# Both parts of the divided values made directly behind the division, in the narrow causal attention layers of a macaron block

## What is computed

```python
def _L0_ffn_ref(x, ln_w, ff_ln_w, wq, wk, wv, wo, wg, w1, w3, w2):
    ...
    q = (h @ wq).reshape(B, S, NHEADS, HEAD_DIM)      # 32 heads of 64
    k = (h @ wk).reshape(B, S, KVHEADS, HEAD_DIM)     # 8 of 64
    v = (h @ wv).reshape(B, S, KVHEADS, HEAD_DIM)
    q, k = _rope(q, k)
    ...
    scores = jnp.where(causal[None, None], scores, jnp.float32(-1e+30))
    attn = jax.nn.softmax(scores, -1)
    o = jnp.einsum('bhqk,bhkd->bqhd', attn, v).reshape(B, S, NHEADS * HEAD_DIM)
    x = x + o @ wo
    ...
```

## Time and profile before

| | us |
|---|---|
| median of three runs | 4106.93 |
| lowest, highest | 4098.98, 4127.73 |
| the profiled execution | 4071.79 |
| its span, first to last instruction | 4070.0 |
| busy: TensorE, VectorE, ScalarE, GpSimd | 3419.7, 2315.2, 1920.3, 1151.3 |
| mean granted TensorE clock | 0.906 of full |

### The profile page before, as it was taken

How to read it: one execution, slowest core, us unless ns; L and a number is a source line. 1 busy time by engine, 2 the same in 40 slices (tenths; PEclk the granted TensorE clock), 3 DMA queues, 4 the chain that set the end, 5 groups by cost and what they waited for, 6 DMA issues and landing times. The chain is left out here.

```text
span 4070.0 us, 63736 instructions
## 1 busy us (share of the span) xinstructions
PE 3419.7 (84%) x21128; PEld 2262.4 (56%) x21130; DVE 2315.2 (57%) x7805; ACT 1920.3 (47%) x5261; POOL 1151.3 (28%) x1088
## 2 busy tenths in 40 slices
PE   6898889888698698988788898888779766999976
PEld 4566666665354333333556666665445445788864
DVE  5555555555343577774555555556434367777765
ACT  4565656645222056666456665655422113555541
POOL 3222322243344200011222222234345442222213
PEclk9899999988799688989899999999889877999996
DMA  2022233011654422120102332311275610000010
GB/s 70 24 68 94 97 125 114 26 56 59 191 90 83 110 52 52 25 43 13 29 23 66 125 114 84 109 32 59 79 182 90 131 38 1 14 14 4 1 31 21
DMA packets 226444, 268.79 MB, mean 66 GB/s; under 512 B 25478, under 2 KB 196424, under 8 KB 225352
## 3 DMA queue, kind: packets, MB, share of 16 engines
q1 hardware_dynamic: 195176, 224.58, 18.1%
q0 software_dynamic: 30944, 40.14, 5.8%
HBM read 129.59 MB, written 134.25 MB: 65 GB/s over the span
## 5 line engine op out<-in xcount | busy, mean ns | idle before, releaser
L1786 ACT ACTIVATE p_prob<-bank,p_small 128x256 f32<-128x256 f32 (+3 forms) x1280 | 646.7, 521 | 151.3 <-DVE p_small L1961 144.2
L1961 DVE CUSTOM_DVE_ANT_0 bank<-bank,p_mask 128x256 f32<-128x256 f32 (+3 forms) x1280 | 581.5, 487 | 240.1 <-PE bank L1525 237.5
L1791 ACT ACTIVATE p_prT<-bank 128x512 f32<-128x512 f32 x752 | 420.4, 602 | 349.9 <-PE bank L1534 349.9
L1525 PE MATMUL bank<-p_k,p_q 64*128 64x256 f32 (+3 forms) x3840 | 537.1, 354 | 10.3 <-ACT p_prob L1786 9.2
L1534 PE MATMUL bank<-g_ident,p_prob 128*128 128x128 f32 x3008 | 431.6, 288 | 68.8 <-DVE p_q L1946 20.7
L2330 POOL TENSOR_TENSOR p_oT_lo<-p_oT,p_oT_hi 128x512 fp32r<-128x512 f32 x128 | 162.3, 1268 | 1068.3 <-ACT p_oT_hi L1799 1057.9
L1534 PEld LDWEIGHTS bank<-g_ident,p_prob 128*128 128x128 f32 x3008 | 339.8, 145 | 152.9 <-DVE p_q L1946 52.7
L1543 PE MATMUL bank<-p_prT,p_v 128*64 128x512 f32 (+1 forms) x1504 | 418.7, 601 | 0.3 <-ACT p_prT L1791 0.3
L1525 PEld LDWEIGHTS bank<-p_k,p_q 64*128 64x128 f32 (+1 forms) x3840 | 346.9, 194 | 113.4 <-issue 70.9
L2319 POOL TENSOR_TENSOR p_tm<-p_rope_a,p_rope_b 128x512 f32<-128x512 f32 x192 | 246.8, 1286 | 517.1 <-DVE p_rope_b L1941 491.6
L2020 DVE TENSOR_REDUCE p_nmax<-bank 128x1 f32<-128x512 f32 x512 | 324.9, 683 | 101.4 <-PE bank L1588 95.7
(11 more groups left out here) (296 smaller groups left out, 6626.8 us busy)
## 6 DMA issues: line engine op xcount, KB each, us to landing
sorted<-p_blank SPq DMA_DIRECT2D x32, 2304.0 KB, 13.1
p_oT<-inverse_saved SPq DMA_DIRECT2D x256, 128.0 KB, 2.9
p_w<-in_L_ffn_w SPq DMA_DIRECT2D x96, 256.0 KB, 4.3
p_h_in<-sorted SPq DMA_DIRECT2D x158, 144.0 KB, 2.7
p_k_st<-k_saved SPq DMA_DIRECT2D x16, 288.0 KB
p_q_st<-q_saved SPq DMA_DIRECT2D x16, 288.0 KB
g_stage<-in_L_ffn_wq SPq DMA_DIRECT2D x8, 512.0 KB, 4.6
g_stage<-in_L_ffn_wo SPq DMA_DIRECT2D x16, 256.0 KB, 6.2
```

Source lines behind the costliest of these rows:

```text
L1525: ins = pe.matmul(h.use.ap[:, 0:n], q[rows, at, :], k[rows, kp, o.g, keys], start=i == 0, stop=i == 2)
L1786: act.activation(s.prob.ap[:, 0:s.o.w], s.use.ap[:, 0:s.o.w], ACT.Exp, bias=sm[:, 0, j:j + 1], scale=-1.0, accum_out=sm[:, 1, j:j + 1]).th ...
L1791: act.activation(s.prT.ap, s.use.ap, ACT.Copy).then_inc(s.use.free[0].sem)
L1961: dve.tensor_tensor_reduce(x, x, A.mask[:, A.mask.shape[1] - o.w:], -1.0, FAR, ALU.add, ALU.min, o.sm.ap[:, 0, h.j:h.j + 1]).then_inc(made)
```

## The change

The step "parts" moves from behind the turns of the first two key tiles to directly behind "divide". The two calls of beside(), the projection of the row tile before (not in the same iteration: `settled` is None there), the scores of heads 2 and 3 and the turns stood between them.

```diff
@@ -626,7 +626,9 @@
                     beside()
                 exponentials()
                 if weighed:
-                    (low_parts if wide else divide)(weighed)
+                    if not wide:
+                        divide(weighed)
+                    low_parts(weighed)
                 if wide:
                     scores(cur, 1)
                 else:
@@ -641,8 +643,6 @@
                     scores(cur, 2, 3)
                 for kt in range(0, min(2, nturn)):
                     turn(prev, kt)
-                if weighed and not wide:
-                    low_parts(weighed)
                 exponentials()
                 if wide:
                     scores(cur, 2)
```

## The result

| | before | after |
|---|---|---|
| Time, us | 4105.7 (4099.0 to 4127.7, 4 runs) | 3994.1 (3989.9 to 4005.8, 4 runs) |
| The profiled execution, us (span) | 4071.8 (4070.0) | 3989.9 (3988.1) |
| Time on a second chip, us | 4061.0 (4053.5 to 4073.2, 9 runs) | 3959.6 (3954.7 to 3970.0, 5 runs) |
| The profiled execution there, us (span) | none taken | 3956.7 (3954.9) |

The change makes the kernel faster: ratio 0.972 (0.968 to 0.977), 112 us, and 0.9755 (0.973 to 0.978) on the second chip, 101 us. Forecast were 78 us and 4029 us in a range of 4000 to 4080: the direction was right, the gain was over two fifths larger, and 3994 lies 6 us under the range.

The account below looks back on a forecast made before the run. TensorE's order was taken to set the pace, its idle stretches being winnable: 117.7 us of waits less 9.4, 5.4, 4, 4.3, 4.2 and 17 gave 73, plus 4 for the clock 77, scaled to 78: 4029 us, range 4000 to 4080.

Parts of the forecast that it names:

- What TensorE waits for: Before the output projection, TensorE waits for the low part, late because ScalarE makes the high part late: 117.7 us, 94 times.
- Position 0's next wait: At the division called position 0, the projection still waits for its bank: 0.8 of 1.28 us won, 4.3 us off the sum.
- The loss at position 2: In 24 units of the first three column blocks, the held q copy delays TensorE's last turn 0.71 us: 17 us lost.
- Rival 3: ScalarE, held by 78 late divisions, becomes what TensorE waits for: at 60% passed on, 28 us slower, 4135 us; chance 0.06.
- The term of the clock: Five low-clock stretches (0.50) follow ordinary position 3 waits, each costing up to 1.7 us: 4 us taken, bound 8.5.
- What a wait is worth: TensorE's waits before the projection were counted at their waiting time, 117.7 us before deductions, with no term for the first matmul.
- The fourth block: At position 2 in the fourth column block, the router's scaling on VectorE holds TensorE anyway: 0 us taken.
- Position 1: The projection's wait of 0.74 us goes, but the q copy limits the win to 0.6 us a unit.
- The idle time itself: TensorE's waits at the projection, 117.7 us, less what stays and the position 2 loss: 73 us won.
- Scaling the sum: The 77 us gain on the profiled run was scaled to the runs' median, 0.86% higher: 78 us.
- The prediction's own sign of being wrong: A narrow causal layer that isn't 35 to 40 us shorter would show the prediction wrong.
- Rival 2: Position 2 costs nothing and all low-clock stretches behind position 3 go: 99 us won, 4007 us; chance 0.13.

Follow-up runs that it names:

- the pair without the stretches: First profile of the kernel before against the changed kernel's on chip B, neither with VectorE or ScalarE standing idle in the fourth blocks; spans differ by 115.1 us.
- the kernel with the copies first: Changed kernel with the parts at position 2 behind the q and k copies, ahead of the scores: 3979.2 us on chip A, 3949.8 us on chip B.
- the pair with the stretches: Also "the pair on A": second profile of the kernel before, on chip A, against the profile after, both with fourth-block idle stretches; 109.1 us less in the narrow layers.

## Why the prediction was right in kind and too small

Right, by its own steps:

- *What TensorE waits for.* The low part was late because ScalarE made the high part behind other copies. With the high part in its new place 84 of 94 waits go, and moving ScalarE's part alone gives the whole gain (3989.9 us).
- *Position 0's next wait.* 0.56 us for the bank of the last rotation; 0.5 was in the sum.
- *The loss at position 2.* The q copy starts 0.69 us later (0.71 reckoned) and the k low part 0.68, so the chain runs as told; but TensorE's wait for it grows by 0.45 us in this unit, to 0.93 and not to 1.2. That ScalarE takes its instructions strictly in order (the Trainium skill, TensorE: Matmul & The Clock Gate, Architectural detail) agrees with this row; it is a cost only where somebody is waiting for what is held.
- *Rival 3*, which needs the holding behind late divisions to reach TensorE: a kernel that holds 0.6 us longer everywhere pays 13 to 22 us.

Wrong, and by how much, in the pair without the stretches (104.7 us measured in the narrow layers, 77 reckoned):

- **The term of the clock**, 4 us with a bound of 8.5. It is the step that failed most. It measured about 20 us in both pairs. The prediction counted five spells behind ordinary position 3 waits; these are the ones in the first three column blocks behind a wait of 1.5 us. The trace of the kernel before has nine behind position 3 waits of 1.5 us or more, and the changed kernel has none, on either chip. So all of them went, and other short ones with them: of spells of 3.4 and 6.8 us there were 23 and are 11, of the longer ones 9 and 10 (on A 25 and 17, 8 and 8). At position 3 alone the time at 0.50 fell by 31 of the 44 us, and TensorE's busy time there by 15. A kernel's time at 0.50 is no measure of its time by itself: the kernel with the copies first has 10 us more of it than the changed one on B, and the same busy time.
- **What a wait is worth**, taken as its idle time alone. The first matmul behind a wait adds 0.26 us more than without one. That term was put at nothing, and it gave about 17 us at the projection and 12 net.
- **The fourth block.** The two fourth blocks together won 31 us. Their idle time fell by 18.4, which is what the sum's waits in them make with the last unit's taken off (14 to 19), and their busy time by 12.4. Position 2 there was taken as 0, because the router's scaling holds TensorE, and won 6.7. A part of that is seen: before the change GpSimd's subtraction ran there at the same time as an instruction of the router on VectorE (L2146), which then took 1.13 us instead of 0.19 and ended with it, and the k low part and TensorE's router step (L1694) stood behind:

```profile
806.09 1.26 POOL L2330 TENSOR_TENSOR p_oT_lo<-p_oT,p_oT_hi 128x512 fp32r<-128x512 f32 x1 [7.88 <-ACT p_oT_hi L1799]
806.27 1.13 DVE L2146 TENSOR_TENSOR p_n_tiles<-p_n_tiles 128x32 f32<-128x32 f32 x1
...
808.09 0.17 PE L1694 MATMUL bank<-p_n_tiles,g_earlier 128*128 128x16 bf16 x1 [3.33 <-DVE p_k L1951]
```

This happens three times in the first profile of the kernel before and one to six times in every kernel whose parts at position 2 stay late in the fourth block, and never in the seven profiles of kernels whose parts there come earlier. TensorE's wait at L1694 for the k low part falls from 14.6 to 10.9 us (on A 18.2 to 10.9, and 14.8 with position 2 alone late).
- **Position 1**, 0.6 us a unit: the q low part moved by 0.90, since the q copy, too, stands behind the projection. In the first three blocks 0.79 us a unit were won, 0.48 of it idle time and 0.31 the projection's first matmul.
- **Position 2 in the first three blocks**: 17 reckoned, 13.5 measured here, 7 in the pair with the stretches.

The idle time itself came out as summed (72.3 against 73), which is partly luck: position 3 gave 35 us of it (39 reckoned) and position 1 15 (20), and position 2 lost 8 and not 17. In the pair on A it fell by 86. In the runs the prediction was for, the gain is 112 us. Scaling the sum by 4106.9/4071.8 was no help: the 35 us between profile and median were not a longer version of the same work but stretches in two blocks that the profile did not have.

The prediction's own sign of being wrong, a narrow layer that isn't 35 to 40 us shorter, came true: from the first to the last division the layers are 55.7 and 49.0 us shorter. The range failed by 6 us. Rival 2 (position 2 free, all low clock gone, 99 us) named the right direction and the right term, but its bound for the clock, 8.5 us, capped it, and position 2 was not free. With a bound from all of the 205 us at 0.50 the range would have begun below 3990.

What stays open: where the stretches of the fourth blocks come from; the rest of what position 2 wins there; and why the waits that went took just these spells at the low clock with them. No run holds the waits and the clock apart.

## What to carry to other kernels

When a change takes short waits out of TensorE's queue at regular places, reckon three things: the idle time; what the first matmul behind each wait adds (here 0.26 us); and the granted clock over the whole stretch, with all the time at the low level as the bound and not a count of a few spells. A wait moved onto an in-order engine costs what its readers lose and not what it holds, so look for the reader first. And when a profile's own time lies outside the range of the timed runs, find out what it lacks before scaling by the median.

## What the runs showed of the hardware

Two chips ran the same kernel 0.9% apart (4099 and 4061 us; two sets on the one, one on the other), at much the same granted clock (about 0.91 over the span on both). The difference lies in the fourth column block of each narrow layer, where GpSimd issues the indirect transfers of the router: there VectorE and ScalarE stand still for up to 7 us at a time on the one chip, 105 us in the four groups of the list under the kernel before, of which some 38 reach the time, and not on the other. With the waits of 1.5 us at position 3 gone, the spells at 0.50 right behind them went too, nine in the pair without the stretches and six in the pair on A; of 44 and 48 us less at 0.50, 31 and 32 lie at position 3.

A projection's first matmul behind a wait adds 0.39 us to TensorE's busy time at the full clock, and 0.12 to 0.13 without a wait. And while GpSimd subtracted 128x512 values (1.26 us), one of VectorE's short instructions with two inputs took 1.13 us instead of 0.19.
